# Second message layer of a two-layer graph network: gathered rows added by the DMA onto edge attributes already in the slot, fp32 messages straight to TensorE

## What is computed

```python
h = jnp.maximum(_layernorm(x, axis=-1), 0.0)
msg = h[src] + edge_attr                                   # 200000 x 64
agg = jax.ops.segment_sum(msg, dst, num_segments=6250)
y = jax.nn.relu(agg @ W1 + b1) @ W2 + b2
x = x + batchnorm(y) * bn_gamma + bn_beta
```

## Time and profile before

| | |
|---|---|
| runs timed | 8547.17, 8472.59, 8500.76 us; median 8500.76 |
| profiled execution, first to last instruction (its span) | 8891.7 us |
| share of the span busy | PE 32%, DVE 56%, ACT 12%, POOL 62% |
| HBM read and written | 467.39 MB, 117.55 MB |

### The profile page before, as it was taken

How to read it: one execution, slowest core, us unless ns; L and a number is a source line. 1 busy time by engine, 2 the same in 40 slices (tenths; PEclk the granted TensorE clock), 3 DMA queues, 4 the chain that set the end, 5 groups by cost and what they waited for, 6 DMA issues and landing times. The chain is left out here.

```text
span 8891.7 us, 55668 instructions
## 1 busy us (share of the span) xinstructions
PE 2871.5 (32%) x13731; PEld 2450.7 (28%) x13731; DVE 5009.9 (56%) x7293; ACT 1027.3 (12%) x1576; POOL 5510.8 (62%) x4913
## 2 busy tenths in 40 slices
PE   1011123544444344425444444353321111122223
PEld 1011123433333333324433343243210111111112
DVE  8999922765656466547656656474732323333334
ACT  3001100111111111101111111010210101111001
POOL 0000066777877767768777778777056666677773
PEclk9975555555555555555555555555565555555555
DMA  1000023333333333324333333336311211111111
GB/s 30 0 0 0 3 73 73 104 93 95 90 93 95 84 87 94 96 61 111 93 94 95 93 98 92 83 99 74 58 46 41 49 45 47 44 49 47 44 44 30
DMA packets 530865, 589.10 MB, mean 66 GB/s; under 512 B 274063, under 2 KB 277263, under 8 KB 530275
## 3 DMA queue, kind: packets, MB, share of 16 engines
q10 hardware_dynamic: 305904, 360.15, 12.9%
q0 software_dynamic: 156672, 160.75, 11.5%
q1 hardware_dynamic: 67954, 64.51, 2.6%
HBM read 467.39 MB, written 117.55 MB: 66 GB/s over the span
## 5 line engine op out<-in xcount | busy, mean ns | idle before, releaser
L819 POOL DMA_INDIRECT rows<-gr_table,row_of x3328 | 3924.5, 1179 | 2133.5 <-issue 1066.9
L831 PE MATMUL bank<-gl_step,hot_t 128*128 128x64 f32 x6720 | 1558.8, 418 | 2582.1 <-DVE parts L1039 1838.4
L831 PEld LDWEIGHTS bank<-gl_step,hot_t 128*128 128x128 f32 x6720 | 1485.0, 328 | 2736.1 <-DVE parts L1039 1972.4
L1306 POOL DMA_INDIRECT message<-h_table,src_sb x1568 | 1565.5, 998 | 757.9 <-issue 471.6
L1010 DVE TENSOR_TENSOR fore<-bank,rows 128x512 f32<-128x512 f32 x416 | 286.0, 688 | 1816.9 <-DMA rows<-gr_table,row_of 1385.0
L1327 PE MATMUL bank<-edge_parts,edge_hot 128*128 128x192 bf16 x1568 | 286.5, 364 | 1803.1 <-DVE edge_parts L1389 1341.0
L838 PE MATMUL bank<-parts,hot_sum 128*128 128x204 bf16 x3328 | 662.5, 376 | 206.1 <-issue 126.3
L1327 PEld LDWEIGHTS bank<-edge_parts,edge_hot 128*128 128x128 bf16 x1568 | 203.8, 141 | 1885.6 <-DVE edge_parts L1389 1395.4
L945 ACT CAST parts<-terms 128x544 bf16<-128x544 f32 x416 | 268.5, 645 | 3028.3 <-DVE terms L1018 2017.0
L838 PEld LDWEIGHTS bank<-parts,hot_sum 128*128 128x128 bf16 x3328 | 516.7, 161 | 276.5 <-issue 139.4
L1033 DVE TENSOR_TENSOR hot_sum<-iota_row,place 128x1024 bf16<-128x1024 f32 x416 | 504.8, 1214 | 0.0
(11 more groups left out here) (264 smaller groups left out, 4163.1 us busy)
## 6 DMA issues: line engine op xcount, KB each, us to landing
place_b<-place_rows ACTq DMA_DIRECT2D x422, 256.0 KB
gr_rows<-rows ACTq DMA_DIRECT2D x416, 256.0 KB
rows_again<-gr_rows ACTq DMA_DIRECT2D x416, 256.0 KB
rows<-gr_table,row_of POOLq DMA_INDIRECT x3328
edge<-in_edge_attr SPq DMA_DIRECT2D x97, 512.0 KB
gl_step<-gl_table ACTq DMA_DIRECT2D x844, 32.0 KB
message<-h_table,src_sb POOLq DMA_INDIRECT x1568
pen_s<-pen_rows ACTq DMA_DIRECT2D x52, 64.0 KB
```

The source lines that it names most:

```text
L819: pool.indirect_dma_start(rows[k][:, g, :], None, m.gr_table[:, :], bass.IndirectOffsetOnAxis(m.row_of[:, tile:tile + 1], 0)).then_inc(s_g ...
L831: last = pe.matmul(bank[slot % LAG][:, g * D:(g + 1) * D], hot_t[slot % LAG][:, g * P:(g + 1) * P], gl_s[slot][:, g // GROUP_TILES, :], st ...
L1306: pool.indirect_dma_start(rows[k][:, e, :], None, m.h2_table[:, :], bass.IndirectOffsetOnAxis(m.src[:, tile:tile + 1], 0)).then_inc(s_gath ...
```

## The change

The attribute load goes straight into the message slots, which now hold whole groups (`V` = 4). POOL waits for that load and issues the same 1,568 gathers with `compute_op=add`, so that each row is added to what lies in its slot. The add, the split and ACT's part go. One-hots become fp32, and PE multiplies them by the 64 fp32 columns of the slot itself. `agg` is a third as wide, its two closing adds go. DVE makes a group's one-hots one group ahead, raises `s_used` when a group's first sum is done (this frees the slot for the next load), and copies a further block's node numbers into PSUM before it compares with them.

```diff
-    rows = [sb(f"message{k}", [P, HALF, D], F32, ctx) for k in range(U)]
-    edge = [sb(f"edge{k}", [P, 2, HALF, D], F32, ctx) for k in range(V)]
+    rows = [sb(f"message{k}", [P, 2, HALF, D], F32, ctx) for k in range(V)]
...
             for h in range(HALVES):
-                k = h % U
-                at_least(pool, s_message, h - U + 1)
+                g, way = h // 2, h % 2
+                pool.wait_ge(s_edge[g % V], (g // V + 1) * 16)
...
-                    pool.indirect_dma_start(rows[k][:, e, :], None, m.h2_table[:, :],
-                                            bass.IndirectOffsetOnAxis(m.src[:, tile:tile + 1], 0)).then_inc(s_gath[k], 16)
+                    pool.indirect_dma_start(rows[g % V][:, way, e, :], None, m.h2_table[:, :],
+                                            bass.IndirectOffsetOnAxis(m.src[:, tile:tile + 1], 0),
+                                            compute_op=ALU.add).then_inc(s_gath[h % U], 16)
...
-                at_least(sp, s_message, 2 * (g - V + 1))
+                at_least(sp, s_used, g - V + 1)
...
-                    done = pe.matmul(out[:, 0:3 * D], one_hot[:, e, :], parts[h % 4][:, e, :, :].rearrange("p w f -> p (w f)"),
+                    done = pe.matmul(out[:, 0:D], one_hot[:, e, :], rows[g % V][:, way, e, :],
...
+                    pe.wait_ge(s_hot_first, h + 1)
+                    pe.wait_ge(s_gath[h % U], (h // U + 1) * 16 * HALF)
...
                 dve.wait_ge(s_first_ps, g + 1)
-                dve.tensor_tensor(sums, sums, bank[g % 2][:, 0:3 * D], ALU.add).then_inc(s_agg, 1)
+                dve.sem_inc(s_used, 1)
+                dve.tensor_tensor(sums, sums, bank[g % 2][:, 0:D], ALU.add).then_inc(s_agg, 1)
...
-                        hot_of(hot_more[:, :, :, :].rearrange("p a t n -> p (a t) n"), m.nodes[:, bass.ds(past * P, P)],
+                        dve.tensor_copy(past_ps, m.nodes[:, bass.ds(past * P, P)]).then_inc(s_past, 1)
...
-            c.link(dve.tensor_tensor(m.agg[:, :, 1, :], m.agg[:, :, 1, :], m.agg[:, :, 2, :], ALU.add))
-            dve.tensor_tensor(m.agg[:, :, 0, :], m.agg[:, :, 0, :], m.agg[:, :, 1, :], ALU.add).then_inc(s_whole, 1)
```

More of the change, by code:

```diff
@@ L213, in build @@
         m.x = sb("x_sb", [P, BLOCKS, D], F32)
-        m.agg = sb("agg", [P, BLOCKS, 3, D], F32)
+        m.agg = sb("agg", [P, BLOCKS, D], F32)
         m.nodes = sb("nodes", [P, BLOCKS * P], F32)
@@ L1161, in _ @@
                       allow_small_or_imprecise_dtypes=True).then_inc(s_layer1, 1)
[L1162 removed]
+            pool.memset(m.agg[:, :, :], 0.0).then_inc(s_layer1, 1)
             pool.tensor_copy(m.dst_f[:, :], m.dst[:, :]).then_inc(s_layer1, 1)
@@ L1269, in messages @@
     attrs = m.t["edge_attr_64"]
-    U, V = 6, 3
+    V = 4
+    U = 2 * V
     HALF = EDGE_TILES // 2
     HALVES = 2 * EDGE_GROUPS
-    SW = HALF * D
-    rows = [sb(f"message{k}", [P, HALF, D], F32, ctx) for k in range(U)]
-    edge = [sb(f"edge{k}", [P, 2, HALF, D], F32, ctx) for k in range(V)]
-    hot = [sb(f"edge_hot{k}", [P, HALF, P], BF16, ctx) for k in range(4)]
-    hot_more = sb("edge_hot_more", [P, 2, HALF, P], BF16, ctx)
-    parts = [sb(f"edge_parts{k}", [P, HALF, 3, D], BF16, ctx) for k in range(4)]
+    rows = [sb(f"message{k}", [P, 2, HALF, D], F32, ctx) for k in range(V)]
+    hot = [sb(f"edge_hot{k}", [P, HALF, P], F32, ctx) for k in range(4)]
+    hot_more = sb("edge_hot_more", [P, EDGE_TILES, P], F32, ctx)
+    numbers_ps, past_ps = (bank[3][:, i * P:(i + 1) * P] for i in range(2))
     s_pool = m.s_pool
@@ L1281, in messages @@
     s_edge = [sem(f"s_edge{k}") for k in range(V)]
-    s_message = sem("s_message")
-    s_hi, s_rest, s_mid, s_parts = sem("s_edge_hi"), sem("s_edge_rest"), sem("s_edge_mid"), sem("s_edge_parts")
-    s_first_ps = sem("s_edge_first_ps")
+    s_used = sem("s_edge_used")
+    s_hot_first, s_first_ps = sem("s_edge_hot_first"), sem("s_edge_first_ps")
     s_hot = sem("s_edge_hot")
@@ L1314, in _ @@
                 k = g % V
-                at_least(sp, s_message, 2 * (g - V + 1))
+                at_least(sp, s_used, g - V + 1)
                 if g == EDGE_GROUPS - 1:
-                    sp.dma_start(edge[k][0:TAIL_PARTS, :, :, :].rearrange("p a t f -> p (a t f)"), tail).then_inc(s_edge[k], 16)
+                    sp.dma_start(rows[k][0:TAIL_PARTS, :, :, :].rearrange("p a t f -> p (a t f)"), tail).then_inc(s_edge[k], 16)
                 else:
-                    sp.dma_start(edge[k][:, :, :, :].rearrange("p a t f -> p (a t f)"),
+                    sp.dma_start(rows[k][:, :, :, :].rearrange("p a t f -> p (a t f)"),
                                  full[g:g + 1, :, :].rearrange("g p f -> p (g f)")).then_inc(s_edge[k], 16)
@@ L1323, in _, with scatter @@
         def _(pe):
-            def scatter(out, one_hot, h, first, last):
+            def scatter(out, one_hot, g, way, first, last):
                 for e in range(HALF):
-                    done = pe.matmul(out[:, 0:3 * D], one_hot[:, e, :], parts[h % 4][:, e, :, :].rearrange("p w f -> p (w f)"),
+                    done = pe.matmul(out[:, 0:D], one_hot[:, e, :], rows[g % V][:, way, e, :],
                                      start=first and e == 0, stop=last and e == HALF - 1)
@@ L1333, in _ @@
                 end = steps_before(pe, g + 1)
[L1334 to L1337, removed]
+                for way in range(2):
+                    h = 2 * g + way
+                    pe.wait_ge(s_hot_first, h + 1)
+                    pe.wait_ge(s_gath[h % U], (h // U + 1) * 16 * HALF)
+                    done = scatter(bank[g % 2], hot[h % 4], g, way, way == 0, way == 1)
+                done.then_inc(s_first_ps, 1)
                 with pe.If_lt(pe.to_reg(before), pe.to_reg(end)), pe.Fori(before, end) as r:
                     pe.wait_ge(s_hot, r + 1)
-                    scatter(bank[2], hot_more[:, 0, :, :], 2 * g, True, False)
-                    scatter(bank[2], hot_more[:, 1, :, :], 2 * g + 1, False, True).then_inc(s_sum_ps, 1)
+                    scatter(bank[2], hot_more[:, 0:HALF, :], g, 0, True, False)
+                    scatter(bank[2], hot_more[:, HALF:EDGE_TILES, :], g, 1, False, True).then_inc(s_sum_ps, 1)
                 before = end
[L1344 to L1350, removed]
         @block.vector
@@ L1357, in hot_of, with hot_first @@
                                          to.unsqueeze(2).to_broadcast([P, n, P]), ALU.is_equal)
+            def hot_first(g):
+                for h in (2 * g, 2 * g + 1):
+                    hot_of(hot[h % 4][:, :, :], numbers_ps, m.dst_f[:, h * HALF:(h + 1) * HALF], HALF
+                           ).then_inc(s_hot_first, 1)
             def add_first(g, steps):
                 blk = dve.value_load(m.first_of[0:1, g:g + 1], min_val=0, max_val=BLOCKS - 1)
-                sums = m.agg[:, bass.ds(blk, 1), :, :].rearrange("p b w f -> p (b w f)")
+                sums = m.agg[:, bass.ds(blk, 1), :].rearrange("p b f -> p (b f)")
                 dve.wait_ge(s_agg, steps + g + 1)
                 dve.wait_ge(s_first_ps, g + 1)
-                dve.tensor_tensor(sums, sums, bank[g % 2][:, 0:3 * D], ALU.add).then_inc(s_agg, 1)
-            dve.tensor_copy(bank[3][:, 0:P], m.iota_row[:, :]).then_inc(s_rel, 1)
+                dve.sem_inc(s_used, 1)
+                dve.tensor_tensor(sums, sums, bank[g % 2][:, 0:D], ALU.add).then_inc(s_agg, 1)
+            dve.tensor_copy(numbers_ps, m.iota_row[:, :]).then_inc(s_rel, 1)
             to_first = m.dst_f[:, :].rearrange("p (g t) -> p g t", t=EDGE_TILES)
@@ L1373, in _ @@
             dve.sem_inc(s_agg, 1)
+            hot_first(0)
             before = steps_before(dve, 0)
             for g in range(EDGE_GROUPS):
[L1376 to L1389, removed]
+                if g:
+                    add_first(g - 1, before)
+                if g + 1 < EDGE_GROUPS:
+                    hot_first(g + 1)
                 end = steps_before(dve, g + 1)
@@ L1398, in _ @@
                                                   "the steps of a group are the blocks past its first")
-                        hot_of(hot_more[:, :, :, :].rearrange("p a t n -> p (a t) n"), m.nodes[:, bass.ds(past * P, P)],
-                               m.dst_f[:, g * EDGE_TILES:(g + 1) * EDGE_TILES], EDGE_TILES).then_inc(s_hot, 1)
+                        dve.tensor_copy(past_ps, m.nodes[:, bass.ds(past * P, P)]).then_inc(s_past, 1)
+                        dve.wait_ge(s_past, r + 1)
+                        hot_of(hot_more[:, :, :], past_ps, m.dst_f[:, g * EDGE_TILES:(g + 1) * EDGE_TILES], EDGE_TILES
+                               ).then_inc(s_hot, 1)
                         dve.wait_ge(s_agg, r + (g + 1))
                         dve.wait_ge(s_sum_ps, r + 1)
-                        sums = m.agg[:, bass.ds(blk, 1), :, :].rearrange("p b w f -> p (b w f)")
-                        dve.tensor_tensor(sums, sums, bank[2][:, 0:3 * D], ALU.add).then_inc(s_agg, 1)
```

(4 more changed lines are left out.)

5 lines of the change are left out of this document (1 added, 4 removed).

## The result

The changed kernel takes 9353.67 us (median of 4 runs, 9337.85 to 9411.9) where the kernel before took 8486.67 (4 runs): 1.101 times as long, 95% interval 1.0958 to 1.1066. The forecast was 8665 us, in a range that ended at 9350.

What follows compares the result with a forecast made beforehand. POOL issuing 1,568 gathers was taken to bound the stage. Span 8891.7 - 84 - 105 - 15 - 7 + 5 = 8686, less 390.9 is 8295; with 370 for the add, 8665 us, range 8210 to 9350.

Steps and rivals of the forecast that it cites:

- (A): The forecast itself: a third address costs POOL 0.1 to 0.47 us per gather, 8450 to 9036 us; chance 0.43.
- (B): Rival: the add is free on POOL because DMA engines do it, 8295 us, between 8189 and 8400; chance 0.35.
- A gather's price on POOL decides the change: Claim that the 2249.0 us stage lasts as long as POOL needs to issue its 1,568 gathers.
- I take half of 472, 236 ns, as a forecast: Added POOL price per accumulating gather, half the 472 ns bound for 128 more addresses; +370 us over 1,568 gathers.
- (C): Rival: POOL makes two passes per gather, 1.5 to 2 times the price, 9036 to 9777 us; chance 0.12.
- -105: POOL's 211.1 us of waits for DVE's add at L1382, half counted as saved; bounds 0 and 211.
- -15: Stage end: DVE's 25.8 us backlog after the last gather shrinks to 10, saving 15 us.
- -84: Gathers lengthened by DVE instructions with two SBUF inputs return to 0.94 us, saving 84 us.
- +5: Stage start: POOL waits for the first attribute load, 0 to 11 us, taken as 5.
- What costs nothing: PE's fp32 tiles (16 in 3.67 us, 536 us in all) and DVE's wider one-hots hide under the gathers.
- (D): Rival: DMA engines become the bound, each row a packet, queue share 12.0% to 96%, 8501 us; chance 0.05.
- (E): Rival: POOL's waits grow as PE's late signals delay `s_used` and the load, 8697 us; chance 0.05.

Runs made afterwards that it cites:

- e1: Changed kernel with plain gathers in place of accumulating ones, attributes left out of the sum: 8488.8 us, 0.986 of the kernel before.
- e2: Kernel before with only its gathers made accumulating, into slots cleared once at the start: 9481.99 us, 1.1021 of the kernel before.
- e3: Changed kernel with each half group's eight gathers in eight forms (row count, row width, with or without add); one execution, add costs 559 ns at 128 rows.
- e4: Kernel before, unchanged, recorded a second time in one execution: span 8589.2 us, time 8591.0 us.
- e6: e5 with DVE's one-hots reading their node numbers from SBUF in place of PSUM: 8746.97 us, 1.0153 of the kernel before.
- e8: Changed kernel with plain gathers; ACT copies attributes to PSUM and DVE adds them onto the gathered rows: 8383.34 us, 0.9877 of the kernel before.
- e5: Changed kernel with plain gathers, attributes in their own slots, PE summing both by two fp32 matmuls per tile: 8687.01 us, 1.0082 of the kernel before.
- e7: Plain gathers, then one accumulating DMA of attributes per group of 16 tiles, in place of the changed kernel's accumulating gathers: 8622.07 us, 1.0013 of before.

## Why the prediction was wrong

Slower was right, and so was the engine; the size was not. The sign rested on the same unsupported choice as the size: no row parted (A) from (B), and below 0.13 us a gather the working gave faster. The steps in their order:

- "A gather's price on POOL decides the change": right. e1 and e2 move the time by that price (in e2 by 883 of 947 us, as said there) and by nothing else of size.
- "I take half of 472, 236 ns, as a forecast": **this step failed.** It was 604 ns, 577 us more than the forecast had for 1,568 of them. It lies above the bound of 472, where the 945 ns were shared out over 256 addresses, and e3 takes away the premise of that bound: about 870 of 992 ns do not depend on the rows. The bound was scaled from a cost that is mostly fixed. What the runs show in its place is a price that is paid mostly per accumulating instruction, about 390 of 559 ns in e3, with 1.3 ns a row on top. The time fell into (C)'s interval, 9036 to 9777, and of (C)'s mechanism, a second pass over the rows, e3 leaves room for that share per row only: the extra would halve with the rows, and it is 559 ns at 128 rows and 491 at 64.
- The runs show 1549 ns for 944, 1.64 times, and by e3 most of the extra does not go by rows. The Trainium skill's rule on two source reads ("Collectives: The Full Stack", section "The bandwidth ceiling: the fold count and why AG ≠ RS ≠ AR") is about the DMA's read descriptors; read across to POOL as three for two it gave 9036. Its direction held, its measure did not.
- "-105" for POOL's waits: should have been 0. e4 shows that waits and excess span were one recording's, so the waits were already in the 390.9 us that the forecast subtracts, and half of them were taken off twice. With it went "-15" for the backlog at the end: e4 ends 84.0 us after the start of its last gather and e1 77.1, so backlog and closing adds together were worth 7, not 22.
- "-84" for the long gathers: right in kind, 110 in e4 against e1. e6 brings them back and e8 keeps them out. "+5" for the first load: the first gather of e1 starts 4.4 us later than that of e4.
- "What costs nothing", PE's fp32 tiles and the wider one-hots: right (e1), but the tiles' own price was misread. The 3.67 us of the earlier trace rows are for 8 tiles, so where the working had 536 us of PE, it was busy for 1039. The 1953 us of gathers covered that too; twice as much, in e5, they did not.
- (D): each row did become a packet, but not one as dear as a packet of eight, and the queue's share is 20.4% where (D) had 96%. (E) fell with the one wait of 87.8 us, (B) with the least duration of 1540 ns.

Put together anew, from recorded spans: e4 to e1 is -113 (-110 in the gathers, -7 at the end, +4 ahead of them), and the add +949. On 8486.67 that makes 9323; measured was 9353.67, and the 31 us left over, 0.3%, are not assigned; e1's interval (0.9818 to 0.9903) is some 36 us wide to either side, so they are within the noise. Without the waits' 105 and the end's 15 the forecast would have been about 8785 by the same 236 ns: it is the price that decided, and a trace in which every gather takes 128 rows could not give it. The range should have reached to (C)'s end for that reason, since its bound of 472 had no row behind its premise.

## What to carry to other kernels

A cost whose least and median agree to 1% over 1,568 instructions may be a loop over equal rows or a fixed cost, and nothing in one trace parts the two: before scaling it, vary the size once. An add that is moved into a transfer is not free when an engine prepares the transfer and is itself the bound: ask how many instructions carry the add (1,568 here, 98 in e7), and whether idle engines can do it (e8). When a recording is some per cent longer than the timed median, its waits, above all those with a releaser outside the core's engines, are suspects; record again before counting them as gain.

## What was not expected of the hardware

- An accumulating gather of 128 rows of 256 bytes took POOL 1549 ns, a plain one 944; by e3 some 390 ns of the difference do not go by rows. Landing took 3.1 us for 2.4, with 144 packets for 32. Whether the 390 ns go into preparing the transfer or into something else of the instruction, no run here parts.
- A contiguous accumulating transfer of 512 KB took POOL 1015 ns and 5.5 us to landing; the load without add, through SP, 3.6.
- A DVE instruction of 2.28 us with both inputs in SBUF held back a gather that began under it, which took 3.04 us and ended 0.83 us after it (e6). Under one with an input in PSUM a gather took 0.94 (e8). The Trainium skill, "SBUF — State Buffer", section "Who interferes with whom", says that a DVE instruction with two SBUF inputs contends with a GpSimd one that reads SBUF, and that the shared pair of ports is an exclusive lock; the trace agrees for the gathers. It does not show the reverse: the one-hots of e6 took 1221 and 2283 ns in the mean, those of e5, with PSUM, 1215 and 2291.
- One recording of the kernel before saw PE's signals up to 42.6 us late and a span 4.6% over the timed median; the second did neither. What did that stays open.
